# Start and counting stage of a graph network kernel: one load queue, multiplications of zeros ahead of x, bases looked at first, the common path right behind the branch, windows of eleven nodes

## The chip, the core and the metric

The kernel runs on one core of one Trainium2 chip. The metric is the device time of one execution in microseconds (us); of the kernel before, three timed runs and one profiled execution are given. Times inside the execution are counted from the start of the profiled span. PE is the matrix engine (PEld its weight loads), DVE the vector engine, ACT the scalar engine, POOL the GpSimd engine and SP the engine that issues most DMAs.

## What is computed

1250 nodes carry 1024 features; 40000 edges (src, dst, type 0 or 1) are sorted by dst. Two graph networks run one after the other, both in float32. Cut to what matters:

```python
# block 0: norm, relational convolution with two edge types, elu, projection, residual
xn  = ln_w * x * rsqrt(mean(x**2) + 1e-6)
out = xn @ W_root + bias                      # 1024 -> 286
for r in range(2):
    w    = (edge_type == r)
    msg  = (xn[src] @ W_rel[r]) * w
    out += segment_sum(msg, dst) / max(segment_sum(w, dst), 1)
x = layernorm(x + x + elu(out) @ wo)
# block 1: layernorm, 1024 -> 512 -> 256, three rounds of h += f(h + segment_sum(h[src], dst)),
#          256 -> 512 -> 1024, layernorms
```

Both blocks gather over the same edges. The kernel therefore counts the edges once into a dense matrix `adj` (source node by destination node, one plane for each type) and multiplies with it.

## The kernel before

The nodes are cut into T = 10 tiles of P = 125. The first stage does two things side by side on PE:

- **Projection.** For each tile, the eight 128-wide blocks of x are transposed (`turn`, L723), ACT copies them out of PSUM with the weight `lnw` (`weigh`, L438), and `products(u, v)` (L729) multiplies block u with 858 columns of `w_all` in two halves of 429. The weights come in four quarters of two blocks each (`load_w`, semaphores `w_in[0]` to `w_in[3]`).
- **Counting.** The edges are cut into G = 80 rows of 500, each in two half rows of 250. For each row DVE makes one-hots of the sources (`lows`, `oh_low`) and of source block, type and destination (`codes`, `oh_code`, L1126), PE multiplies them (`count`, L715, four matmuls, 240 columns each), and DVE adds the two results to `adj` at the columns of the half row's least destination (L1181 and L1185, loaded into registers by `bases`, L1154). The window behind that base has W = 12 nodes, C = T * W, R * C = 240 columns. Whether every half row fits its window is looked at on the chip (`gaps`, `signs`, L1143 to L1148) and gives `bign`; if one does not, DVE and later PE take another path over `adj_x`, the same matrix in plain float32.

The order of the start is written out by hand. SP issues x of tile 0, `lnw8`, quarter 1 of the weights, dst, src, type, quarters 2 and 3, and x of tile 1; ACT issues quarter 0. POOL makes the iotas `iota_r`, `iota_i`, `iota_c` and then zeroes parts of `adj`; DVE makes `ident`, `iota_l` and its own parts of `adj`, then works on the edges as they land: least dst of each half row (L1087), `e_low` (L1092), `e_code` (L1097), greatest dst (L1099). PE transposes tile 0 and runs `products(0..7, 0)`; ahead of `products(6, 0)` it transposes `e_low`, and ahead of `products(7, 0)` x of tile 1, `e_code` (L708) and the bounds (L780). DVE then copies `edge`, `mini`, `ends` (L1104 to L1107), makes the one-hots of rows 0 and 1, looks at the windows (L1143 to L1149), loads `bign` (L1334) and branches (L1335): the body of `If(big > 0)` stands first in the program and the usual path behind `Else`. What follows both, up to the loop over chunks, stands behind the two.

In the loop over pairs of tiles (`tile_of_1` on PE and on DVE, `Fori(0, T // 2 - 1)`, four passes) each tile has nine count rows. PE's order is row u, products u, for u from 0 to 7; behind row 4 it transposes the next x and has row 5 at once. DVE does rows in order and ahead of its u = 3 the two `y_lo` instructions of the tile before (`low_part`, L1164, L1165). PE waits for one-hots (`onehots`), DVE for counts (`counts_mm`); both are two rows apart through two buffers. When DVE is done it sets `adj_done` (L1225), SP then issues `cb_b`, and the aggregation begins (L864 and L866, single pass float32r).

Of the kernel before, what the change touches and what calls it, by code (L numbers as in the profile page):

```python
# [25 lines left out]
P = 125  # L26
# [9 lines left out]
J = 4  # L36
# [5 lines left out]
W = 12  # L42
# [14 lines left out]
def graph_kernel(nc, x, src, dst, typ, ln_w, w_rel, w_root, conv_b, wo, g_in, b_in, w1, b1, w2, b2,  # L57
                 wa, ba, wb, bb, ng, nb, wd1, bd1, wd2, bd2, g_out, b_out, out):
    with ExitStack() as ctx:
# [113 lines left out]
        def spread(a):  # L173
# [11 lines left out]
        lnw_ps, lnw_set, lows_ready, far_copied, ends_set, far_ready = (  # L185
            sem("lnw_ps"), sem("lnw_set"), sem("lows_ready"), sem("far_copied"), sem("ends_set"), sem("far_ready"))
# [73 lines left out]
        def _(sp):  # L260
# [3 lines left out]

            load_x(0, 0)
            sp.dma_start(lnw8[:], ln_w.rearrange("(k p) -> k p", p=128)).then_inc(lnw_in, 16)
# [87 lines left out]
        def _(pool):  # L354
# [347 lines left out]
        def _(pe):  # L702
# [54 lines left out]

            pe.wait_ge(small_set, 4)
# [4 lines left out]
            turn(1, 0)  # L763
            for u in range(KD):
# [290 lines left out]
        def _(dve):  # L1055
# [4 lines left out]
            dve.memset(zero[:], 0.0).then_inc(small_set, 1)  # L1060
            dve.memset(mini[:], 0)
            dve.memset(edge[:], 0.0)
            dve.memset(farC[:], 0.0).then_inc(prep, 1)
            dve.wait_ge(iotas, 2)
            dve.tensor_scalar(ident[:], iota_r[:], iota_i[:, 0:1], None, ALU.is_equal).then_inc(small_set, 1)
            dve.tensor_copy(iota_l[:], iota_r[0:P].rearrange("p (n o) -> p n o", o=1).broadcast_to([P, LOW, JH]))
            dve.wait_ge(small_set, 4)
            for b in range(5):
# [18 lines left out]
            dve.tensor_reduce(bounds[:, 0:H], halves(dst_i), AX.X, ALU.min)  # L1087
            dve.wait_ge(src_in, 16)
# [402 lines left out]
```

## Time and profile before

| | us |
|---|---|
| three timed runs, median (lowest to highest) | 604.26 (603.21 to 604.66) |
| profiled execution, device time | 605.02 |
| its span | 603.2 |
| PE busy in the span | 574.2 |
| DVE busy | 393.1 |
| ACT busy | 213.8 |
| POOL busy | 103.0 |

The profiled execution is 0.76 us above the median of the runs; 1.8 us of it lie outside the span. Busy times are modelled for PE, since matmuls are pipelined: the time from one start to the next is the better measure of what one costs. In the slices of the profile each of the 40 digits stands for 15.1 us.

### The profile page before, as it was taken

The page shows a single profiled execution, that of the slowest core. Times are in us where ns is not written, and L with a number is a line of the kernel's source. Part 1 is how long each engine was busy: PE and PEld are TensorE (multiplying, and loading weights), DVE is VectorE, ACT ScalarE, POOL GpSimd, SP SyncE. Part 2 cuts the span into 40 slices and gives each one's busy share as a digit, 9 for nine tenths or more (in the row PEclk, how much of TensorE's full clock was granted, in tenths as well). Part 3 has the DMA queues.
Part 4 walks back from the last instruction along what each step waited for, and adds up shares of the span by engine and source line. Part 5 has one row for each costly group of instructions (what it writes and reads, how often), then busy time and mean ns, then how long its engine had stood idle before and what let it go on. Part 6 is the DMA issues. An engine that isn't in the chain of part 4 may idle for free.

```text
span 603.2 us, 8370 instructions
## 1 busy us (share of the span) xinstructions
PE 574.2 (95%) x2575; PEld 395.9 (66%) x2575; DVE 393.1 (65%) x998; ACT 213.8 (35%) x456; POOL 103.0 (17%) x98
## 2 busy tenths in 40 slices
PE   4969999999999999999999999999999999999992
PEld 2535555555558686766788888886877867455540
DVE  7569999999985788888733202015848848655454
ACT  6612233222312446465322222002223224175555
POOL 9300000000000000003054333400211230041230
PEclk9979999999999999999999999999999999999997
DMA  9401111001103121114720000320010100021223
GB/s 259 134 11 35 34 34 35 13 21 34 34 1 89 35 69 35 61 43 118 213 93 0 1 0 0 115 105 1 1 36 0 35 0 2 1 68 34 70 68 102
DMA packets 20848, 30.73 MB, mean 51 GB/s; under 512 B 5393, under 2 KB 15107, under 8 KB 20816
## 3 DMA queue, kind: packets, MB, share of 16 engines
q1 hardware_dynamic: 19846, 29.19, 16.5%
q10 hardware_dynamic: 970, 1.13, 0.7%
q8 instruction: 17, 0.28, 0.2%
q14 instruction: 15, 0.12, 0.1%
HBM read 25.20 MB, written 5.12 MB: 50 GB/s over the span
## 4 chain that ended last, share of the span: by engine, by line
PE 86%; DVE 5%; issue 3%; DMA 2%; DVEq 2%; ACT 1%; POOL 0%; ACTq 0%
PE banks L729 16%; PE banks L918 12%; PE banks L1004 11%; PE banks L835 11%; PE banks L805 5%; PE banks L715 5%; PE banks L940 4%; PE banks L930 4%; PE banks L864 4%; PE banks L866 4%; PE banks L845 3%; PE banks L994 3%; PE banks L809 2%; DVEq L1154 1%; PE banks L820 1%
## 5 line engine op out<-in xcount | busy, mean ns | idle before, releaser
L729 PE MATMUL banks<-w_all,xnT 128*125 128x429 f32 x320 | 131.9, 537 | 2.0 <-DMA w_all<-in_L_gnn_W_rel 2.0
L729 PEld LDWEIGHTS banks<-w_all,xnT 128*125 128x125 f32 x320 | 55.7, 193 | 34.5 <-issue 31.4
L835 PE MATMUL banks<-hT,w_s 128*128 128x250 f32 x320 | 68.7, 375 | 0.4 <-DVE hT L1309 0.3
L835 PEld LDWEIGHTS banks<-hT,w_s 128*128 128x128 f32 x320 | 60.3, 189 | 9.1 <-issue 2.2
L715 PEld LDWEIGHTS banks<-oh_code,oh_low 125*128 125x128 bf16 x320 | 30.7, 98 | 43.9 <-issue 29.1
L715 PE MATMUL banks<-oh_code,oh_low 125*128 125x240 bf16 x320 | 48.3, 273 | 7.8 <-DVE oh_code L1126 7.8
L864 PE MATMUL banks<-y_hi,adj 125*125 125x288 f32 x200 | 55.2, 304 | 0.4 <-DVE small L1225 0.4
L866 PE MATMUL banks<-y_lo,adj 125*125 125x286 f32 x200 | 53.6, 295 | 0.0
L1126 DVE TENSOR_TENSOR oh_code<-iota_c,edge 125x960 bf16<-125x960 f16 x82 | 53.3, 650 | 0.0
L375 POOL TENSOR_SCALAR xh<-x_first,small 125x1024 f32<-125x1024 f32 x6 | 7.4, 1236 | 261.1 <-DVE adj L1253 261.0
L1309 DVE TENSOR_SCALAR hT<-banks,g_c,b_c 128x125 f32<-128x125 f32 x60 | 19.4, 399 | 45.6 <-PE banks L820 45.2
L918 PE MATMUL banks<-adj,h_hi 125*128 125x250 f32 (+1 forms) x180 | 48.2, 366 | 0.0
L918 PE MATMUL banks<-adj,h_lo 125*128 125x250 f32 (+1 forms) x180 | 45.6, 353 | 0.0
L1181 DVE TENSOR_TENSOR adj<-adj,banks 125x240 f32 x80 | 32.1, 401 | 18.2 <-PE banks L715 13.0
L1004 PE MATMUL banks<-wd_s,dT 128*125 128x512 f32 x96 | 42.7, 592 | 0.0
L864 PEld LDWEIGHTS banks<-y_hi,adj 125*125 125x125 f32 x200 | 37.1, 186 | 7.2 <-issue 6.1
L438 ACT ACTIVATE xnT<-banks,lnw 128x125 f32<-128x125 f32 x80 | 22.6, 377 | 52.5 <-PE banks L723 52.5
L380 POOL TENSOR_TENSOR h_lo<-h,h_hi 125x256 fp32r<-125x256 f32 x30 | 21.8, 732 | 107.6 <-ACT h_hi L570 107.6
L866 PEld LDWEIGHTS banks<-y_lo,adj 125*125 125x125 f32 x200 | 37.3, 186 | 0.0
L805 PE MATMUL banks<-wo_s,yT 128*125 128x512 f32 x80 | 36.0, 592 | 0.0
L1122 DVE TENSOR_TENSOR oh_low<-iota_l,edge 125x512 bf16<-125x512 f16 x82 | 34.3, 418 | 0.2
L918 PEld LDWEIGHTS banks<-adj,h_hi 125*128 125x128 f32 x180 | 29.8, 189 | 5.5 <-issue 1.4
(187 smaller groups left out, 912.2 us busy)
## 6 DMA issues: line engine op xcount, KB each, us to landing
xt<-in_x SPq DMA_DIRECT2D x15, 448.0 KB
out_x<-ot SPq DMA_DIRECT2D x9, 448.0 KB
w_s<-in_L_gnn_W SPq DMA_DIRECT2D x5, 512.0 KB, 6.1
xn<-in_x SPq DMA_DIRECT2D x5, 448.0 KB
wd_s<-in_L_gnn_Wd SPq DMA_DIRECT2D x1, 2048.0 KB, 12.8
w_all<-in_L_gnn_W_rel SPq DMA_DIRECT2D x6, 286.0 KB, 8.6
wo_s<-in_L_gnn_wo_weight SPq DMA_DIRECT2D x1, 1024.0 KB, 6.6
w_all<-in_L_gnn_W_root SPq DMA_DIRECT2D x3, 286.0 KB, 7.9
```

Source lines behind the costliest of these rows:

```text
L715: ins = pe.matmul(pb[:, b, q * R * C:(q + 1) * R * C], oh_low[:, b, q, :, j], oh_code[:, b, q, :, j], start=(j == 0), stop=(j == JH - 1))
L729: ins = pe.matmul(pb[0:P, 2 + 2 * v + n, 0:FH], xnT[:, u], w_all[:, u, n * FH:(n + 1) * FH], start=(u == 0), stop=(u == KD - 1))
L805: pe.matmul(pb[0:P, 5 + q], yT[:, i], wo_s[:, i, q * 512:(q + 1) * 512], start=(i == 0), stop=False)
L835: ins = pe.matmul(pb[:, 4 + f % 2, 0:2 * P], w1_s[:, k, f * 128:(f + 1) * 128], hT[:, k], start=(k == 0), stop=(k == KD - 1))
L864: pe.matmul(pb[0:P, b + r, 0:F + 2], mine, y_hi[:, s, r * (F + 2):(r + 1) * (F + 2)].bitcast(kind), start=(s == 0), stop=False)
L866: ins = pe.matmul(pb[0:P, b + r, w0:w0 + F], mine, y_lo[:, s, r * F:(r + 1) * F].bitcast(kind), start=False, stop=(s == T - 1))
L918: ins = pe.matmul(pb[:, 3 * f + c, 0:n], part[:, s, f * 128:(f + 1) * 128], adj[:, 0, s, c0:c0 + n], start=(s == 0 and part is h_hi), stop ...
L930: ins = pe.matmul(pb[:, 3 * f + c, 0:n], wa_s[:, k, f * 128:(f + 1) * 128], zT[:, k, c0:c0 + n], start=(k == 0), stop=(k == K2 - 1))
L1004: ins = pe.matmul(pb[0:P, 2 + 2 * u + q], (dT, dT_odd)[c % 2][:, k, u * P:(u + 1) * P], wd2_s[:, k, q * 512:(q + 1) * 512], start=(k == 0) ...
L1122: return dve.tensor_tensor(oh_low[:, b], both(iota_l, LOW), spread_out(edge[:, 0], g, LOW), ALU.is_equal)
L1126: return dve.tensor_tensor(oh_code[:, b], both(iota_c, R * C), spread_out(code, g, R * C), ALU.is_equal)
L1181: dve.tensor_tensor(place, place, window(b, 0), ALU.add).then_inc(first_added, 1)
```

## The change

- **Loads.** SP issues all first loads, in the order `lnw8`, x of tile 0, quarters 0 and 1, dst, src, type, quarters 2 and 3, x of tile 1. ACT issues none of them.
- **Zeros on PE.** DVE sets `oh_code[:, 0]` to zero early; PE multiplies it with itself, 5 matmuls of 440 columns ahead of its first waits and 4 more behind the transposes of tile 0.
- **Start of DVE and POOL.** DVE makes `ident` and `iota_l` ahead of the zeroing of `mini`, `edge` and `farC`; POOL waits for `ident` ahead of `iota_c`; DVE zeroes 7 blocks of plane 1 in place of 5, POOL two fewer.
- **Bases first.** The greatest dst comes right behind the least; PE transposes the bounds ahead of `products(5, 0)` into banks 4 and 5; DVE copies `mini` and `ends` and looks at the windows while it waits for PE's transposes of the edges, not behind the first one-hots.
- **Branch.** `bign[0, 1]` says that all windows fit. `If(fine > 0)` has the usual path as its first body, and what followed both bodies (`into_encoder`) stands in each of them.
- **Window.** W is 11 in place of 12: 220 columns in each count matmul, 880 elements in place of 960 for each partition in `codes`, 220 in place of 240 in each addition to `adj`.

```diff
-W = 12
+W = 11
@@ SP
+            sp.dma_start(lnw8[:], ln_w.rearrange("(k p) -> k p", p=128)).then_inc(lnw_in, 16)
             load_x(0, 0)
-            sp.dma_start(lnw8[:], ln_w.rearrange("(k p) -> k p", p=128)).then_inc(lnw_in, 16)
+            load_w(sp, 0)
             load_w(sp, 1)
@@ POOL
+            pool.wait_ge(small_set, 4)
             pool.iota(iota_c[:], ...)
-            pool.wait_ge(small_set, 3)
-            for r, b in [(1, b) for b in range(5, T)] + [(0, 8), (0, 9)]:
+            for r, b in [(1, b) for b in range(7, T)] + [(0, 8), (0, 9)]:
@@ ACT
-            load_w(act, 0)
@@ PE
+            def warm(n, bank):
+                flat = oh_code[:, 0].rearrange("p q c j -> p (q c j)")
+                for _i in range(n):
+                    pe.matmul(pb[:, bank, 0:2 * R * C], flat[:, 0:128], flat[:, 0:2 * R * C], start=True, stop=True)
+            pe.wait_ge(warm_set, 1)
+            warm(5, 5)
             pe.wait_ge(small_set, 4)
             ...
             turn(0, 0)
             turn(1, 0)
+            warm(4, 5)
             for u in range(KD):
...
+                if u == 5:
+                    pe.wait_ge(bounds_ready, 1)
+                    for i in range(2 * H):
+                        ins = pe.transpose(pb[0:1, 4 + i // H, i % H * G:(i % H + 1) * G], bounds[:, i:i + 1], ident[0:G, 0:G])
+                    ins.then_inc(bounds_ps, 1)
...
-                    turn_edges(1, e_code)
-                    for i in range(2 * H):
-                        ins = pe.transpose(pb[0:1, i // H, (J + i % H) * G:(J + i % H + 1) * G], bounds[:, i:i + 1], ident[0:G, 0:G])
-                    ins.then_inc(edges_ps, 1)
+                    turn_edges(1, e_code).then_inc(edges_ps, 1)
@@ DVE
+            dve.memset(oh_code[:, 0], 0.0).then_inc(warm_set, 1)
+            dve.wait_ge(iotas, 2)
+            dve.tensor_scalar(ident[:], ...).then_inc(small_set, 1)
+            dve.tensor_copy(iota_l[:], ...)
             dve.memset(mini[:], 0)
             dve.memset(edge[:], 0.0)
             dve.memset(farC[:], 0.0).then_inc(prep, 1)
-            for b in range(5):
+            for b in range(7):
...
             dve.tensor_reduce(bounds[:, 0:H], halves(dst_i), AX.X, ALU.min)
+            dve.tensor_reduce(bounds[:, H:2 * H], halves(dst_i), AX.X, ALU.max).then_inc(bounds_ready, 1)
...
             dve.reciprocal(small1[:, 4:5], small1[:, 2:3]).then_inc(xn_rstd, 1)
+            dve.wait_ge(bounds_ps, 1)
+            (copies of mini and ends, then gaps, signs)
+            dve.tensor_scalar(bign[0:1, 1:2], signs[0:1, 0:1], 0.0, None, ALU.is_ge)
+            dve.tensor_scalar(bign[0:1, 0:1], signs[0:1, 0:1], 0.0, None, ALU.is_lt).then_inc(big_ready, 1)
             dve.wait_ge(edges_ps, 1)
             (copies of edge; the one-hots of rows 0 and 1; the look at the windows is gone from behind them)
...
-            with dve.If(big > 0):
-                dve.memset(adj_x[:], 0.0).then_inc(wide_set, 1)
-                ...
-            with dve.Else():
-                counted(adj)
-                after_counts()
-                aggregated(adj)
-            (the common lines up to adj_full)
+            fine = dve.value_load(bign[0:1, 1:2], min_val=0, max_val=1)
+            with dve.If(fine > 0):
+                counted(adj)
+                after_counts()
+                aggregated(adj)
+                into_encoder()
+            with dve.Else():
+                dve.memset(adj_x[:], 0.0).then_inc(wide_set, 1)
+                ...
+                into_encoder()
```

## Rows read from the trace of the kernel before

**Rows 1.** The page: the final chain by engine, and the costliest group of additions (count, busy, mean ns)

```profile
PE 86%; DVE 5%; issue 3%; DMA 2%; DVEq 2%; ACT 1%; POOL 0%; ACTq 0%
...
L1181 DVE TENSOR_TENSOR adj<-adj,banks 125x240 f32 x80 | 32.1, 401 | 18.2 <-PE banks L715 13.0
```

**Rows 2.** Chain of waits, 0 to 46 us: start, length, what (DVEq: its sequencer)

```profile
2.19 7.70 DMA w_all<-in_L_gnn_W_rel
...
10.03 10.93 PE banks L729 x24
20.96 0.40 PE banks L708 x4
...
23.67 0.29 PE banks L780 x4
...
23.98 0.89 DVE edge L1104 x2
...
25.53 0.42 DVE oh_low L1122
...
27.42 0.23 DVE gaps L1143
...
29.18 0.03 issue
...
30.26 2.84 issue
...
34.22 0.10 DVE adj L1181
...
35.89 0.98 PE banks L715 x4
...
43.36 0.43 PE banks L715 x4
```

**Rows 3.** Timeline of PEld, 13 to 14 us: start, length, instruction, idle before it

```profile
13.02 0.33 PEld L729 LDWEIGHTS banks<-w_all,xnT 128*125 128x125 f32 x1 [0.38 <-issue]
13.74 0.33 PEld L729 LDWEIGHTS banks<-w_all,xnT 128*125 128x125 f32 x1 [0.38 <-issue]
```

**Rows 4.** Stretches: length; busy PE, PEld, DVE, ACT, POOL; granted clock, DMA share, GB/s

```profile
15.00:16.00 1.00, 1.00 (x4) 0.56 (x3) 0.99 (x2) 1.00 (x2) 1.00 (x2) 1.00 1.09 367
...
35.00:41.00 6.00, 5.11 (x13) 2.75 (x14) 5.15 (x13) 0.00 (x0) 0.00 (x0) 0.50 0.00 0
42.00:46.00 4.00, 4.00 (x24) 2.67 (x23) 3.22 (x10) 1.13 (x4) 0.00 (x0) 1.00 0.03 6
```

**Rows 5.** DMA, 8.84 to 8.90 us (issue; us to landing) and 31.0 to 31.5 us (queue; packets)

```profile
w_all<-in_L_gnn_W_rel SPq DMA_DIRECT2D x1, 286.0 KB, 10.4
...
q14 instruction: 1, 0.01, 6.2%
```

**Rows 6.** Timeline of 0 to 24 us, POOL and DVE

```profile
1.13 3.05 POOL L359 IOTA iota_c<- 125x480 f16 x1
...
2.40 1.85 DVE L1065 TENSOR_SCALAR ident<-iota_r,iota_i 128x128 f32<-128x128 f32 x1
...
12.09 0.67 DVE L1087 TENSOR_REDUCE bounds<-dst_i 80x2 f32<-80x500 int32 x1 [2.34 <-DMA dst_i<-in_dst]
...
17.65 0.14 DVE L1101 RECIPROCAL small<-small 125x1 f32<-125x1 f32 x1
```

**Rows 7.** Timeline around and inside the loop, and a DVE row at 323.93 us

```profile
29.32 1.61 PE L729 MATMUL banks<-w_all,xnT 128*125 128x429 f32 x4
...
39.34 0.66 DVE L1165 SCALAR_TENSOR_TENSOR y_lo<-banks,small,y_hi 125x429 f32 x1
...
109.31 0.65 DVE L1126 TENSOR_TENSOR oh_code<-iota_c,edge 125x960 bf16<-125x960 f16 x1
...
110.02 0.60 PE L715 MATMUL banks<-oh_code,oh_low 125*128 125x240 bf16 x4 [0.24 <-DVE oh_code L1126]
...
323.93 1.35 DVE L1309 TENSOR_SCALAR hT<-banks,g_c,b_c 128x125 f32<-128x125 f32 x4 [14.25 <-PE banks L820]
```

More of the change, by code:

```diff
@@ L1060, in _ @@
             dve.memset(zero[:], 0.0).then_inc(small_set, 1)
+            dve.memset(oh_code[:, 0], 0.0).then_inc(warm_set, 1)
+            dve.wait_ge(iotas, 2)
+            dve.tensor_scalar(ident[:], iota_r[:], iota_i[:, 0:1], None, ALU.is_equal).then_inc(small_set, 1)
+            dve.tensor_copy(iota_l[:], iota_r[0:P].rearrange("p (n o) -> p n o", o=1).broadcast_to([P, LOW, JH]))
             dve.memset(mini[:], 0)
@@ L1096, in _ @@
                 part = slice(q * JH * P, (q + 1) * JH * P)
-                dve.scalar_tensor_tensor(e_code[:, part], dst_i[:, part], bounds[:, q:q + 1], e_mark[:, part],
-                                         ALU.subtract, ALU.add)
-            dve.tensor_reduce(bounds[:, H:2 * H], halves(dst_i), AX.X, ALU.max).then_inc(edges_ready, 1)
+                ins = dve.scalar_tensor_tensor(e_code[:, part], dst_i[:, part], bounds[:, q:q + 1], e_mark[:, part],
+                                               ALU.subtract, ALU.add)
@@ L1100, in _ @@
+            ins.then_inc(edges_ready, 1)
             dve.wait_ge(xn_sd, 1)
             dve.reciprocal(small1[:, 4:5], small1[:, 2:3]).then_inc(xn_rstd, 1)
-            dve.wait_ge(edges_ps, 1)
-            for f in range(2):
-                dve.tensor_copy(edge[:, f, 0:G], pb[0:P, f, 0:J * G].rearrange("p (j g) -> p g j", j=J))
-            dve.tensor_copy(mini[:].rearrange("o (g q) -> o q g", q=H)[:, :, 0:G],
-                            pb[0:1, 0, J * G:(J + H) * G].rearrange("o (q g) -> o q g", q=H))
@@ L1107, in _ @@
-            dve.tensor_copy(ends[:].rearrange("o f (g q) -> o f q g", q=H),
-                            pb[0:1, 0:2, J * G:(J + H) * G].rearrange("o f (q g) -> o f q g", q=H)).then_inc(codes_ready, 1)
+            dve.wait_ge(bounds_ps, 1)
+            dve.tensor_copy(mini[:].rearrange("o (g q) -> o q g", q=H)[:, :, 0:G],
+                            pb[0:1, 4, 0:H * G].rearrange("o (q g) -> o q g", q=H))
+            step(dve.tensor_copy(ends[:].rearrange("o f (g q) -> o f q g", q=H),
+                                 pb[0:1, 4:6, 0:H * G].rearrange("o f (q g) -> o f q g", q=H)))
@@ new lines, in _, with sift @@
+            crowds = [0]
+            def sift(ins):
+                ins.then_inc(crowd, 1)
+                crowds[0] += 1
+                dve.wait_ge(crowd, crowds[0])
+            NG = G * H
+            NS = NG - SPAN
+            dve.memset(gaps[0:1, NG - 1:NG], 0.0)
+            dve.tensor_tensor(gaps[0:1, 0:NG - 1], ends[0:1, 0, 1:NG], ends[0:1, 0, 0:NG - 1], ALU.subtract)
+            dve.scalar_tensor_tensor(gaps[0:1, NG:NG + NS], ends[0:1, 0, SPAN:NG], -float(W), ends[0:1, 0, 0:NS], ALU.add, ALU.subtract)
@@ new lines, in _ @@
+            sift(dve.scalar_tensor_tensor(gaps[0:1, NG + NS:2 * NG + NS], ends[0:1, 0], float(W - 1), ends[0:1, 1], ALU.add, ALU.subtract))
+            dve.tensor_reduce(signs[0:1, 1:2], gaps[0:1, NG + NS:2 * NG + NS], AX.X, ALU.min)
+            sift(dve.tensor_reduce(signs[0:1, 0:1], gaps[0:1, 0:2 * NG + NS], AX.X, ALU.min))
+            dve.tensor_scalar(bign[0:1, 1:2], signs[0:1, 0:1], 0.0, None, ALU.is_ge)
+            dve.tensor_scalar(bign[0:1, 0:1], signs[0:1, 0:1], 0.0, None, ALU.is_lt).then_inc(big_ready, 1)
@@ L1109, in _ @@
+            dve.wait_ge(edges_ps, 1)
+            dve.tensor_copy(edge[:, 0, 0:G], pb[0:P, 0, 0:J * G].rearrange("p (j g) -> p g j", j=J))
+            dve.tensor_copy(edge[:, 1, 0:G], pb[0:P, 1, 0:J * G].rearrange("p (j g) -> p g j", j=J)).then_inc(codes_ready, 1)
             dve.wait_ge(codes_ready, 1)
```

55 lines of the change are left out of this document (19 added, 36 removed).

## Prediction

> **What bounds the kernel now.** I read the page's chain first: PE holds 86% of it [rows 1], so only time in which PE waits, runs at its low clock level or does needless columns can be won, and whatever is won early moves everything behind it. Then the chain of waits over the first 46 us [rows 2], to see where PE is not the one that works. Three places stand out. First, PE's first product starts at 10.03, when quarter 0 of the weights has landed (2.19 + 7.70 = 9.89). Second, from 23.98, when DVE begins to copy the turned edges, the chain is DVE's up to 35.89, when PE gets the one-hots of count row 2. The largest piece in it, 2.84 us from 30.26, is no instruction at all. PE has nothing left from about 30.9 on (the last products of row 1 start at 29.32 and take 1.61 [rows 7]). Third, the clock: two loads of weights in the first products are 0.72 apart [rows 3], yet 24 records took 10.93 in all, which is 0.46 each, so the clock rose on the way; the clock column shows no half level there, the spacing does. Behind the idle 5 us it shows 0.50 (1.2 GHz) over the whole of 35 to 41 us, and 1.00 (2.4 GHz) from 42 on [rows 4]. Inside the loop PE is the bound but for one place a tile: row 5 comes right behind row 4, and PE gets it at 110.02, as DVE's codes end (109.31 + 0.65 = 109.96) [rows 7].
>
> **Loads and zeros.** In one queue quarter 0 no longer shares the DMA engines with quarter 1. The engines carry 367 GB/s while SP alone feeds them [rows 4], so one queue is enough to fill them. Quarter 0 is 858 KB and x is 500 KB; at that rate they take 3.8 us, so with the start at about 2.2 and one to two us of completion quarter 0 lands between 7 and 9, not at 9.89. But the bytes of all loads together are unchanged, and the last piece of quarter 3 landed at 8.85 + 10.4 = 19.25 (it is the issue of that window) [rows 5], against the 20.96 at which PE is ready for block 6 [rows 2]. So of this part at most 20.96 - 19.25 = 1.7 us can reach the end: what is late next is quarter 3. The first x is issued behind `lnw8` and nothing from ACT runs beside it, for which I add 0.3: block 6 at 19.6, a gain of 1.4 (bounds: -0.3, if PE starts no earlier, to 2.0). The nine multiplications of zeros cost at most 9 x 440 columns at 1.2 GHz = 3.3 us of PE, five while it would wait for x, four while ACT copies xnT and quarter 0 is under way; if that cover failed (quarter 0 in ahead of the last of them) they would cost PE up to 1.5 us, which the slack before quarter 3 takes up. What they win in clock is hidden by the same wait: I book nothing for it.
>
> **DVE's and POOL's start.** `ident` took 1.85 us and ended at 4.25, as POOL's `iota_c` did (1.13 + 3.05 = 4.18) [rows 6]: it was held, not working. Now POOL waits for it, so `ident` is early; but the 3.05 of `iota_c` then run beside `iota_l` and the zeroing, and such a hold (up to 1.6, what `ident` took over 0.25 or so) may only move there. The zeroing grows by two blocks, which I put at 1 us each from the element count; DVE has 2.34 of idle ahead of L1087 [rows 6]. So dst is met 0 to 1.5 late. The Trainium skill (GPSIMD Engine Reference, the table of section 1) says that POOL shares its SBUF interfaces with DVE, in conflict with DVE's two-port modes or two SBUF inputs; the trace agrees with the 1.85 of `ident`, and by the rule the upper end, 1.5 late, is the one to expect. From there to `e_code` and the reciprocal it takes 17.79 - 12.09 = 5.7, so up to 19.3, and the look at the bases (below, 2.4) ends by 21.7; its cover is PE, which hands over the edges at 22.3. No cost, with 0.6 us to spare.
>
> **Bases first.** From block 6 to the hand-over PE took 23.98 - 20.96 = 3.02; the four transposes of the bounds (0.29) [rows 2] go to block 5, ahead of quarter 3's landing, so 2.73 stay: DVE starts copying at 19.6 + 2.73 = 22.35, not 23.98. A gain of 1.65. Off DVE's path there go the copies of `mini` and `ends` (24.87 to 25.53: 0.66) and the look (27.42 to 29.18: 1.76).
>
> **The branch.** From 30.26 DVE does nothing for 2.84 us, behind L1335 and ahead of the loop, and in that time the queue of instruction reads moves one packet [rows 2, 5]: it jumps over the body of `If` and the code there has to be read. With the usual path first nothing is jumped over. I take 0.0 for it (bounds 0.0 and 2.84). The Trainium skill has the rule (Runtime: NRT & Kernel Launch, Instruction fetch mechanics: reading ahead is sequential, and a taken branch out of the window waits for a DMA), and the trace agrees with its 2.84. The jump is not gone: it stands behind `into_encoder` now, over the other body. There DVE waits 14.25 us for PE [rows 7], which hides it; without that cover it would cost its 2.84.
>
> **Eleven nodes.** A count of 240 columns takes 0.43 for four matmuls [rows 2]; 20 columns less at 2.4 GHz are 0.008 each, 0.033 a row (bounds 0, if the loads of weights set the spacing, and 0.036, a twelfth). A twelfth of `codes` (0.65) [rows 7] would be 0.054 and of an addition (0.401) [rows 1] 0.033; both have a fixed part, so I take 0.04 and 0.02: a DVE row gets 0.08 shorter (0 to 0.12).
>
> **Sum to row 5 of tile 1.** DVE from first copy to first addition: 34.22 - 23.98 = 10.24, less 0.66, 1.76, 2.84 and 0.08 for two shorter codes = 4.9. So the first addition comes at 27.25, not 34.22. Row 2's codes end 1.6 later (35.84 - 34.22, less 0.08, rounded): PE gets row 2 at 28.85, not 35.89. PE itself needs until some 28.6 for rows 0 and 1 with their products (what ended at 30.93, earlier by 1.65 and by the copies of 0.66): it stands still for 0.2 or 0.3 us, not 5, and the 6 us at half clock [rows 4] go as well. From there DVE sets the pace: three rows of 1.5 and the two `y_lo` instructions (0.66 and about 0.2) give row 5 at 28.85 + 4.5 + 0.85 = 34.2. Before it was 43.36 [rows 2]. **9.2 us.**
>
> **Sum from there.** In each of seven more tiles three count rows and two DVE rows lie between PE's count 2 and count 5, where DVE is the slower: 2 x 0.08 = 0.16 there, and 7 x 0.033 = 0.23 on the other rows: 0.39 x 7 = 2.7. The last 12 rows give 0.4. **3.1 us** (bounds 1.2, if only DVE gets shorter, and 4). Behind the loop nothing changes but positions in the program.
>
> 12.3 us in all. The profiled execution of 605.02 becomes 592.7; it lies 0.76 above the median, so the median of 604.26 becomes **592.0**.
>
> **Rivals.**
> A, the forecast: 592.0, by itself 589.5 to 594.3 (loads -1.4 or +0.4, window 1.2 or 4). Chance 0.72.
> B, the wait at the branch stays (the loop's head has to be read in any case). PE then stands 3.1 us: +2.8, and if the clock falls behind that, as it did behind 5 us, half of the 6 us again: 594.8 to 597.6. For it: the 2.84 is only known next to a taken branch. Against: the next instruction is the next in sequence. 0.12.
> C, a back edge of DVE's loop has to read code. Before there was no such wait in the loop. The body moves inside the program, and where it crosses one block of code more than is kept, each of three back edges costs 2.84, less its lead over PE of half a row or so, 0.8: +6, 598. 0.06.
> D, loads: the single queue brings quarter 3 or x of tile 1 later, or DVE is held beyond its spare 0.6: each us is one us, 593 to 596. 0.07.
> E, slower: windows of eleven are too few. A single half row of 250 edges that reaches over 12 nodes decides it: `fine` is 0, everything takes the `adj_x` path. That is 20 blocks of zeros more (some 20 us) and 400 aggregation matmuls in plain float32: a float32 matmul of 429 columns is two records of 0.36 (half of 0.72 [rows 3]), so one of 288 is 0.48, against 288 columns at 2.4 GHz, 0.12, in one pass: +144. About 750 us. Against: 32 edges a node make 250 edges span eight nodes, and over the reference's dst the largest distance inside a half row is 9, where 10 are allowed. 0.01. The remaining 0.02 is for gains lost in ways I don't see, to within 0.3% of before.
>
> **How the numbers follow.** The range of 589.3 to 597.6 takes in A, B and D, over 8 in 10. A measurement of this kernel tells 0.3% (1.8 us) from no change. All cases but E and the remainder are faster: 0.96; same 0.02; slower 0.02, which gives E a little for mishaps like it.
>
> **What would show it.** In the profile after: quarter 0's landing and the first product (8 to 9 us), and PE waiting for quarter 3 close to 19.5; `edge` copied at 22.3, the look at the bases ahead of it; no gap of 2.84 before the first addition to `adj`, at 27.2; row 2's count at 28.9 with a clock of 1.00 throughout; a tile of the loop 0.4 shorter than before; no idle PE where DVE jumps behind `into_encoder`. The forecast is wrong if DVE meets dst after 14, if instruction reads appear in the loop, or if a half clock shows between 28 and 35 us.

## The result: 593.0 us, forecast 592.0

The changed kernel took 593.0 us (592.87 to 594.06, four runs), the kernel before beside it 604.04: a ratio of 0.982, interval 0.9807 to 0.9832. The profiled execution was the longest of the four, 594.06 with a span of 592.0; the span before was 603.2, so the traces have 11.2 us to share out.

The page after, its final chain, the queues of instruction reads and two of the groups that the window of eleven nodes touches (the additions to `adj` answer to [rows 1]):

```profile
q14 instruction: 15, 0.12, 0.1%
...
PE 86%; DVE 4%; DMA 2%; issue 2%; DVEq 2%; SPq 1%; ACT 1%; POOL 0%
...
L715 PE MATMUL banks<-oh_code,oh_low 125*128 125x220 bf16 x320 | 44.7, 260 | 2.8 <-DVE oh_code L1159 2.8
...
L1196 DVE TENSOR_TENSOR adj<-adj,banks 125x220 f32 x80 | 30.6, 383 | 15.1 <-PE banks L715 14.1
```

The timeline of PE up to the copies of the edges, which answers to the first part of [rows 2] (start, length, instructions, idle time before them):

```profile
2.11 2.02 PE L762 MATMUL banks<-oh_code 125*128 125x440 bf16 x5 [2.11 <-DVE oh_code L1072]
...
7.19 1.63 PE L762 MATMUL banks<-oh_code 125*128 125x440 bf16 x4
8.84 3.12 PE L729 MATMUL banks<-w_all,xnT 128*125 128x429 f32 x8
12.17 3.15 PE L729 MATMUL banks<-w_all,xnT 128*125 128x429 f32 x8 [0.21 <-DMA w_all<-in_L_gnn_W_rel]
16.43 1.68 PE L729 MATMUL banks<-w_all,xnT 128*125 128x429 f32 x4 [1.11 <-DMA w_all<-in_L_gnn_W_rel]
...
19.87 0.66 PE L708 MATMUL banks<-ident,e_low 80*125 80x80 f32 x4
```

Behind the zeros eight matmuls of the products take 3.12 us, 0.39 each and not the 0.72 of [rows 3], so they run at 2.4 GHz from the first on; but PE then stands twice, because it now meets the quarters of the weights as they land. The next answer is the chain of waits from the copies of the edges on, which answers to the second part of [rows 2]:

```profile
22.88 0.49 DVE edge L1140
23.37 0.41 DVE edge L1141
23.80 0.04 DVE oh_low L1155
...
23.90 0.55 DVEq L1367
24.45 0.32 DVE oh_code L1159
...
24.81 0.57 PE banks L715 x4
```

There is no pause of 2.84 us any more, and L1367, the load of the branch's flag into a register, is done by DVE's sequencer at 24.45, while the one-hots still run. The clock over the stretch that stood at 0.50 before [rows 4] (length; busy time of PE, PEld, DVE, ACT, POOL; granted clock, DMA share, GB/s):

```profile
28.00:34.00 6.00, 5.78 (x30) 3.36 (x29) 5.64 (x15) 1.47 (x5) 0.00 (x0) 1.00 0.13 42
```

**Where the 11.2 us come from.** Two instructions cut the span into three parts: the start of DVE's fifth addition (DVE adds twice for each row; the first of the two is counted, so this is that of row 4. PE begins row 5 of tile 1 behind it, 0.05 us in the changed kernel and 0.20 in the kernel before) and that of the eightieth, in the last row. Up to the fifth it is 43.16 before and 33.79 after: 9.37 gained. From the fifth to the eightieth 138.76 and 137.07: 1.69 gained. From the eightieth to the end of the span 421.28 and 421.14: 0.14. The forecast had 9.2, 3.1 and 0. This is one trace of each kernel: in a second one of the changed kernel the span is 591.2 and the fifth addition starts at 32.75, so the gain up to it is 10.4 there and 12.0 in all.

### The profile page after: what moved, and what is told of

Same layout as the page of the kernel before. It is cut to its first block, busy times and chain, and to the rows that moved or that the text cites. A ratio compares the mean times of both kernels' runs of the same rounds, so it can differ in the third digit from the quotient of the medians.

```text
span 592.0 us, 8385 instructions
## 1 busy us (share of the span) xinstructions
PE 571.5 (97%) x2584; PEld 394.8 (67%) x2584; DVE 391.1 (66%) x1002; ACT 213.9 (36%) x456; POOL 100.8 (17%) x90
## 4 chain that ended last, share of the span: by engine, by line
PE 86%; DVE 4%; DMA 2%; issue 2%; DVEq 2%; SPq 1%; ACT 1%; POOL 0%
PE banks L729 14%; PE banks L929 12%; PE banks L1015 12%; PE banks L846 12%; PE banks L816 5%; PE banks L715 5%; PE banks L951 4%; PE banks L941 4%; PE banks L875 4%; PE banks L877 4%; PE banks L856 3%; PE banks L1005 3%; PE banks L820 2%; DVEq L1169 1%; DMA w_all<-in_L_gnn_W_rel 1%
## 5 line engine op out<-in xcount | busy, mean ns | idle before, releaser
L729 PE MATMUL banks<-w_all,xnT 128*125 128x429 f32 x320 | 129.1, 526 | 1.3 <-DMA w_all<-in_L_gnn_W_rel 1.3
L729 PEld LDWEIGHTS banks<-w_all,xnT 128*125 128x125 f32 x320 | 53.8, 188 | 31.8 <-issue 30.8
L1159 DVE TENSOR_TENSOR oh_code<-iota_c,edge 125x880 bf16<-125x880 f16 x82 | 50.0, 610 | 0.0
L715 PE MATMUL banks<-oh_code,oh_low 125*128 125x220 bf16 x320 | 44.7, 260 | 2.8 <-DVE oh_code L1159 2.8
L1196 DVE TENSOR_TENSOR adj<-adj,banks 125x220 f32 x80 | 30.6, 383 | 15.1 <-PE banks L715 14.1
L438 ACT ACTIVATE xnT<-banks,lnw 128x125 f32<-128x125 f32 x80 | 22.6, 378 | 43.7 <-PE banks L723 43.7
```

The source lines that it names most:

```text
L715: ins = pe.matmul(pb[:, b, q * R * C:(q + 1) * R * C], oh_low[:, b, q, :, j], oh_code[:, b, q, :, j], start=(j == 0), stop=(j == JH - 1))
L729: ins = pe.matmul(pb[0:P, 2 + 2 * v + n, 0:FH], xnT[:, u], w_all[:, u, n * FH:(n + 1) * FH], start=(u == 0), stop=(u == KD - 1))
L1159: return dve.tensor_tensor(oh_code[:, b], both(iota_c, R * C), spread_out(code, g, R * C), ALU.is_equal)
L1196: dve.tensor_tensor(place, place, window(b, 0), ALU.add).then_inc(first_added, 1)
```

## The experiments

All are edits to the changed kernel, but for one to the kernel before; "neither" and the last row undo or change two things at once, the others one. The table gives the timed median, the ratio to the kernel before on the same chip with its interval, and from each trace the start of the edges' first copy, of the fifth addition, and the time from the fifth to the eightieth.

| kernel | us (lowest to highest) | ratio | copy | fifth | to 80th |
|---|---|---|---|---|---|
| before | 604.04 | 1 | 23.98 | 43.16 | 138.76 |
| changed | 593.0 (592.87-594.06) | 0.982 [0.9807, 0.9832] | 22.88 | 33.79 | 137.07 |
| changed, again | 594.08 (593.2-595.01) | 0.9841 [0.9822, 0.9859] | 21.83 | 32.75 | 137.04 |
| old branch order | 594.56 (594.15-595.45) | 0.9843 [0.9824, 0.9862] | 21.37 | 34.48 | 136.31 |
| bases looked at late | 597.3 (596.52-597.96) | 0.9879 [0.9861, 0.9897] | 22.30 | 37.66 | 137.05 |
| window of twelve | 595.74 (595.3-596.07) | 0.9856 [0.9839, 0.9874] | 21.50 | 32.61 | 139.63 |
| before + branch order | 600.98 (600.69-601.82) | 0.9947 [0.9928, 0.9966] | 24.37 | 39.28 | 138.97 |
| no zeros | 593.34 (592.86-593.99) | 0.9826 [0.9812, 0.9839] | 23.06 | 33.97 | 137.02 |
| two queues | 593.01 (592.66-593.06) | 0.982 [0.9806, 0.9833] | 22.35 | 33.26 | 137.05 |
| neither | 594.25 (593.71-595.53) | 0.9845 [0.9825, 0.9865] | 23.51 | 34.43 | 137.04 |
| shifted loop | 593.02 (591.42-596.06) | 0.9825 [0.9798, 0.9853] | 22.53 | 33.44 | 136.36 |
| shifted loop, again | 592.24 (591.6-593.08) | 0.9805 [0.9787, 0.9823] | 21.75 | 32.66 | 136.33 |
| subtraction at row 6 | 590.6 (590.19-593.33) | 0.9781 [0.9766, 0.9795] | 24.67 | 35.22 | 134.62 |
| the same, twelve | 593.16 (592.52-594.68) | 0.9825 [0.9805, 0.9844] | 21.27 | 32.00 | 137.26 |

How to read it: the last column repeats to 0.05 us (six traces of the loop as it is in the changed kernel gave 137.02 to 137.07), so it settles tenths. The column of the copies does not: with the start of the program unaltered it lies between 21.27 and 24.67, since the first loads land when they will (`dst` is met at 11.97 to 14.05). What an edit does between copy and fifth addition is therefore read as their difference, 10.91 in the changed kernel (33.79 - 22.88), 10.92 in its repeat (which was expected at 592.7 to 593.3 us and took 594.08). The ratios are coarser: the changed kernel itself gave 0.982 on one chip and 0.9841 on another, 1.3 us apart, so a difference of two ratios from different chips that is smaller than this says little by itself.

**The branch's order undone.**

```diff
-            fine = dve.value_load(bign[0:1, 1:2], min_val=0, max_val=1)
-            with dve.If(fine > 0):
-                counted(adj)
+            big = dve.value_load(bign[0:1, 0:1], min_val=0, max_val=1)
+            with dve.If(big > 0):
+                dve.memset(adj_x[:], 0.0).then_inc(wide_set, 1)
...
+            with dve.Else():
+                counted(adj)
```

> The changed kernel with the order of the branch put back (wide body first, usual path behind Else, common lines behind both); all else as changed. Theory 1 (the 2.84 us is the read of code behind a taken branch, and DVE sets the pace from its first addition to row 5): the gap of 2.8 us is back ahead of the first addition (26.4 becomes 29.2 us), PE waits some 2 us for row 2 at full clock, row 5 comes 2.6 us later than 33.84; 593.0 becomes 595.6. Theory 2 (the gap of before only existed because the sequencer had waited for the windows to be looked at; now it runs ahead and the read of code hides behind the one-hots): 593.0 to 594.0. Theory 3 (the wait is long enough for the clock to fall): 598 or more.

The chain of waits of this kernel, from the jump (L1350) to the first addition:

```profile
23.30 0.07 DVEq L1350
23.37 0.13 issue
23.50 0.61 DVE oh_code L1159
24.11 2.07 issue
26.18 0.05 DVEq L1207
...
27.30 0.10 DVE adj L1196
```

The gap is back at the same place with everything else in the new form, 2.07 us here. But it is only the part that nothing covers: DVE's sequencer jumps ahead of the second codes, is done with that at 23.37, and its next step is at 26.18, 2.81 us later; 0.74 of it lie beside the one-hots. In the kernel before it was 2.84 (30.26 to 33.10) and all of it bare, since the flag came last. So the jump has the same price in both, and what is seen of it depends on what DVE still has queued. From the copy to the fifth addition it is 13.11 instead of 10.91: 2.2 us. But the loop is 0.76 shorter than the changed kernel's, 136.31 against 137.07; 2.2 - 0.76 = 1.4, and the two ratios differ by 0.0023, 1.4 us (by 0.0002 with the repeat's ratio). The mechanism is the first theory's, the clock did not fall, and its 595.6 us was too high: part of the jump is covered, which the second theory had for the whole of it, and the loop is shorter. The jump's cost is shown in the trace; that the new order also costs something in the loop was not in either theory, and led to the shifted loop below.

**The branch's order alone, in the kernel before** (the same edit the other way round, with `bign`'s second flag).

> The kernel before with the order of the branch alone changed. Theory 1 (2.84 us of reading code go; PE's idle stretch of 5 us shrinks to 2.1 and the clock stays at 1.00, so DVE and no longer PE's half clock sets row 5): row 5 at 38.5 in place of 43.36, 604.0 becomes 599.2. Theory 2 (the clock falls all the same): 2.84 only, 601.2. Theory 3 (the read of code is only moved): 604.0.

From copy to fifth addition 14.91, where the kernel before has 19.18: 4.27 gained in the trace, against 3.2 us in the time (604.77 x (1 - 0.9947)), of an interval of 2.1 to 4.4. Of the 4.27, 2.78 are at the first addition (31.83 - 24.37 = 7.46 behind the copy instead of 10.24) and 1.49 between it and the fifth, since PE stands still for so much less that its clock stays up. That is the first theory; its row 5 at 38.5 came at 39.39, and the time, 600.98, is nearer to the second theory's 601.2, whose fallen clock the trace does not have. Below are PE's row 2 and the window around it, in this kernel:

```profile
33.75 0.60 PE L715 MATMUL banks<-oh_code,oh_low 125*128 125x240 bf16 x4 [2.44 <-DVE oh_code L1126]
```

```profile
30.00:35.00 5.00, 2.56 (x11) 1.25 (x10) 3.02 (x8) 1.23 (x3) 0.00 (x0) 1.00 0.17 64
35.00:40.00 5.00, 4.14 (x24) 2.60 (x23) 4.93 (x14) 1.13 (x4) 0.00 (x0) 1.00 0.02 5
```

**The look at the bases put back behind the one-hots.** The bounds' transposes stand behind the codes' again, and copies, `gaps` and `signs` where they stood:

```diff
-                if u == 5:
-                    pe.wait_ge(bounds_ready, 1)
...
-                    turn_edges(1, e_code).then_inc(edges_ps, 1)
+                    turn_edges(1, e_code)
+                    for i in range(2 * H):
+                        ins = pe.transpose(pb[0:1, 4 + i // H, i % H * G:(i % H + 1) * G], bounds[:, i:i + 1], ident[0:G, 0:G])
+                    ins.then_inc(edges_ps, 1)
```

> The changed kernel with the bounds transposed behind the edges again, mini and ends copied behind edge, and the look at the windows behind the one-hots of rows 0 and 1. Theory 1 (each piece lies on DVE's path to the first addition, and the sequencer can no longer load bign ahead): 0.3 for PE's transposes, 0.66 for the copies, 1.8 for the look, 1.1 for the load of bign behind it = 3.8 us later at the first addition, of which 1 us was spare on PE's side at row 2 but none at row 5: 596.5 to 596.8. Theory 2 (the sequencer's part overlaps in either order): 2.7 us, 595.7.

PE's row 2 in this kernel, and then the window around it:

```profile
31.69 0.91 PE L715 MATMUL banks<-oh_code,oh_low 125*128 125x220 bf16 x4 [2.56 <-DVE oh_code L1137]
32.41 2.78 PE L729 MATMUL banks<-w_all,xnT 128*125 128x429 f32 x4
```

```profile
30.00:35.00 5.00, 3.31 (x8) 1.78 (x9) 4.75 (x13) 0.00 (x0) 0.00 (x0) 0.66 0.02 5
```

It took 597.3 us, where the theories had 596.5 to 596.8 and 595.7. The timed difference to the changed kernel is 0.0059, 3.6 us; in the traces the way from copy to fifth addition is 15.36 instead of 10.91, 4.45 longer, and the loop is the same. The first addition comes 7.80 behind the copy (30.10 - 22.30) instead of 3.53: 4.27 of the 4.45 are there already, near the 3.8 of the first theory. The copies of `mini` and `ends` and the look are 0.6 and 1.8 of them; the other 1.9 are the load of the flag, the branch and the load of the bases, which ran beside the one-hots in the changed kernel and now stand behind the look. PE is idle for 2.56 us ahead of row 2, and here the clock does fall: the count takes 0.91 instead of 0.56 and the four matmuls behind it 2.78 instead of 1.61. That is 1.5 us of PE, but little of it is new: from the first to the fifth addition it takes 7.56 us, and 7.18 in the kernel with the old branch order, where the clock stays up and DVE sets the pace. So the fallen clock cost some 0.4. The look is worth more than its own length (2.4 with the copies) above all because the sequencer's work behind it gets covered too.

**The window of twelve nodes** in the changed kernel (`W = 12`).

> The changed kernel with windows of twelve nodes. Theory 1 (0.027 a row on PE, and next to nothing on the stretch where DVE sets the pace, since its sequencer does): 1.6 us in the loop and 0.1 or 0.2 ahead of it, 594.7 to 594.8. Theory 2 (the prediction's term of 3.1 us was right and something else took 1.5 us of it back): 596.1.

The loop takes 139.63 instead of 137.07, 2.56 us. The ratios differ by 0.0036, 2.2 us, and the time, 595.74, lies between the two theories. The 2.56 is less than the 3.1 of the forecast, and it is 0.87 more than the 138.76 of the kernel before, which has the same window. So two things had happened to that term at once: it was set 0.5 too high, and something in the loop took 0.87 back.

**The loop shifted by sixteen instructions.** They do nothing and stand where DVE waits for PE in any case:

```diff
+            for k in range(16):
+                dve.memset(gaps[0:1, 2 * NG + NS + k:2 * NG + NS + k + 1], 0.0)
             dve.wait_ge(edges_ps, 1)
```

> The changed kernel with sixteen one-element zeroings on VectorE ahead of its wait for the codes' transposes, where it idles 1.64 us: they do nothing but move everything behind them, the counting loop too, by sixteen instructions in VectorE's program. In the changed kernel every second tile takes 16.54 us instead of 16.40, and VectorE's sequencer pauses 0.12 us more between two rows of it, at row 3; with the branch's old order the same loop takes 16.40 us for all tiles. First theory (the pause is the crossing from one fetched block of instructions to the next, and lies at the one row where VectorE has no slack): shifted by sixteen instructions it falls more than a row earlier, where VectorE waits for TensorE anyway, all pitches become 16.40, row 5 of tile 1 to the end of the counting shortens from 138.6 to about 137.9 us, and the time is 592.1 to 592.5. Second theory (the odd and even tiles differ for another reason, as the buffers that they use): pitches and time stay, 592.7 to 593.3 us. Third: the shift brings the crossing to a worse place, 593.5 or more, which would speak for the first theory's mechanism too.

> The changed kernel with the sixteen one-element zeroings ahead of the counting loop, a second time, because its first timing was scattered (591.4 to 596.1 us) while its trace had all pitches at 16.40 us and 0.72 us less from row 5 of tile 1 to the last addition. First theory (the trace is right and the 0.72 us reaches the end): 592.0 to 592.5 us, ratio to the kernel before 0.001 below the unaltered changed kernel's. Second (what is gained in the loop is waited for again behind it): the same as the unaltered one within 0.2 us.

The chain of waits in the fourth tile, first of the changed kernel, then of the shifted one, from PE's row to the sequencer's last step ahead of DVE's addition (L1194 and L1196 there are L1196 and L1198 here):

```profile
78.70 0.41 PE banks L715 x4
...
79.14 0.04 DVEq L1194
79.18 0.17 issue
79.35 0.05 DVEq L1196
```

```profile
78.00 0.41 PE banks L715 x4
...
78.43 0.04 DVEq L1196
78.47 0.05 issue
78.52 0.05 DVEq L1198
```

The pause of 0.17 between these two steps of the sequencer is 0.05 in the shifted kernel. At row 5 PE's idle time shows what becomes of it, in the same order of kernels:

```profile
83.56 0.56 PE L715 MATMUL banks<-oh_code,oh_low 125*128 125x220 bf16 x4 [0.33 <-DVE oh_code L1159]
```

```profile
82.72 0.57 PE L715 MATMUL banks<-oh_code,oh_low 125*128 125x220 bf16 x4 [0.20 <-DVE oh_code L1161]
```

The tiles of the loop now take 16.39 to 16.42 us, where every second took 16.51 to 16.54 and the second tile 16.76. In that one the pause at the same step is longer:

```profile
46.00 0.41 issue
```

This is 0.36 more than 0.05, and with 0.12 in each of the three passes behind it makes 0.72. The way to the eightieth addition is 136.36 and 136.33: 0.72 us less, in both traces, for sixteen instructions that compute nothing. The loop's position in the program is what matters; the rival about buffers falls, as the buffers were left as they were. The pause itself is not gone in the shifted kernel: it stands at another step now, nearly two rows earlier (L1202 to L1161, 0.21 us instead of 0.07 ahead of 75.19, and so in each later pass; 0.46 in the first, ahead of 42.63), where it costs nothing. In the times the two measurements, 0.9825 and 0.9805, stand against 0.982 and 0.9841 of the unaltered kernel: in the mean 0.0016 or 0.9 us lower, but the intervals overlap, so the times alone would not have shown it (593.02 misses the 592.1 to 592.5 of the first theory, 592.24 meets its 592.0 to 592.5). That the pause is the step from one block of fetched code to the next, the first theory, fits with its moving by a fixed number of instructions, and with its being longer in the first pass, in which reads of 8 KB each move (q14: 0.12 MB in 15; packets at 42.5 and 47.1). But none moves in the fourth tile, so the cause was not shown, only the dependence on position.

**The subtraction ahead of row 6.**

```diff
-                    if u == 3:
+                    if u == 6:
                         low_part(t - 1, 1 - v)
```

> The changed kernel with one edit inside the counting loop: VectorE subtracts the high parts of tile t (low_part) ahead of row 6 of the next tile instead of ahead of row 3. In the changed kernel TensorE idles 0.20 us (odd tiles) to 0.56 and 0.33 us (even tiles) ahead of row 5, because VectorE is behind by then. First theory (the two subtractions of 0.4 and 0.6 us meet VectorE with the least slack at row 3, and later in the tile they would be hidden): the stall ahead of row 5 goes, row pitch stays 1.85 us, 0.2 to 0.33 us for each of 8 tiles, 2.0 to 2.3 us in all, 590.7 to 591.0 us. Second theory (VectorE's work of a tile is what sets the pace, wherever it stands): the stall moves to row 8 of the tile or to row 0 of the next, and the time stays at 592.7 to 593.3. Third (the products of the next tile wait for y_lo, so that a late subtraction makes TensorE wait): slower, 594 or more.

This is the fastest kernel: 590.6 us, although its profiled execution met the latest loads of all. The loop takes 134.62 instead of 137.07, 2.45 us less, and from the copy to the fifth addition it is 10.55 instead of 10.91. This is the first theory, with its time (590.7 to 591.0). The stretch from 40 to 160 us of the changed kernel, and the same of this one:

```profile
40.00:160.00 120.00, 117.88 (x554) 70.32 (x553) 106.33 (x282) 35.69 (x105) 0.00 (x0) 1.00 0.10 30
```

```profile
40.00:160.00 120.00, 120.00 (x566) 71.45 (x565) 110.17 (x292) 35.70 (x105) 0.00 (x0) 1.00 0.10 30
```

PE has no idle time left there, so the wait did not move to another row: two subtractions of 0.4 and 0.7 us stood at the one place where DVE had no slack.

**The same with a window of twelve.**

> The changed kernel with the subtraction ahead of row 6 (as in the variant that took 590.6 us and left TensorE no idle time in the counting) and, besides, the window of twelve nodes again. In the unaltered changed kernel the window of twelve cost 2.6 us from row 5 of tile 1 on. First theory (the window's worth is TensorE's: a count of 0.43 instead of 0.40 us per row, 75 rows left, and nothing of VectorE's since it has slack here): 75 x 0.027 = 2.0 us more than the variant with eleven, 592.5 to 592.9 us. Second (VectorE's longer additions and one-hots, 0.1 us a row, run into the bound again with twelve): 593.1 us or more, with idle time of TensorE back in the rows ahead of row 5 or 8.

137.26 against 134.62: 2.64 us, 0.0044 or 2.7 us in the ratios. PE is never idle in either, so all of it is PE's, and my number for the first theory was too low: I had taken 0.027 us per row from two rounded pitches, while 2.64 over 75 rows is 0.035. That is four matmuls of 20 columns at 2.4 GHz, 0.033, as the forecast had it. The longer instructions of DVE cost nothing of their own; the second theory falls, with its time met.

**The start: no zeros, two queues, neither.** The first leaves L762 and its zeroed operand out. The second puts the loads back:

```diff
-            sp.dma_start(lnw8[:], ln_w.rearrange("(k p) -> k p", p=128)).then_inc(lnw_in, 16)
             load_x(0, 0)
-            load_w(sp, 0)
+            sp.dma_start(lnw8[:], ln_w.rearrange("(k p) -> k p", p=128)).then_inc(lnw_in, 16)
             load_w(sp, 1)
...
+            load_w(act, 0)
```

> The changed kernel without TensorE's multiplications of zeros ahead of and behind the transposes of x (TensorE idles instead). First theory (TensorE waits for the DMA of each quarter of the weights in any case, and the third quarter's landing sets when the edges' transposes run): the first products run at the half clock, 0.72 us each instead of 0.36, for some us, but TensorE has 1.1 us of idle time ahead of quarter 2 and 0.7 ahead of quarter 3, which takes most of it up: 592.8 to 593.3 us. Second theory (half-clock products delay the look at the bases, or TensorE comes late to quarter 3): edge copies 1 to 2 us later and the same in the time, 594 to 595 us.

> The changed kernel with the first quarter of the weights fetched by ScalarE's queue again, the rest by SyncE's, as before the change. First theory (one queue lets the quarters land in the order in which they are wanted, and the third one earlier; the prediction put this at 1.4 us at block 6 of the first tile): edge copies 1 to 1.4 us later, 594.0 to 594.4 us. Second theory (the DMA engines share the same bytes either way, and what the first kernel lost was the order of x and the edge arrays, not the second queue): within 0.3 us of the changed kernel, 592.7 to 593.3.

> The changed kernel with both edits at its start undone: the first quarter of the weights on ScalarE's queue again, and no multiplications of zeros. Undone one at a time they cost nothing that could be measured (593.3 and 593.0 us). First theory (each makes up for the other's lack: with two queues the quarters land early but x is late and its products start at the half clock; with one queue TensorE waits for quarters in any case): without both, the first products start near 10.0 us at the half clock, the low codes' transposes run 1 to 1.4 us later than with both, and the time is 593.7 to 594.4 us. Second theory (neither has an effect on the start): within 0.3 us of the unaltered one.

Taken out alone, neither costs anything that can be measured (0.9826 and 0.982 against 0.982). For the zeros this is the first theory; for the queues it is the second theory's number, but what makes up for the second queue is the zeros. With two queues PE is handed x later, at 6.02 us instead of 5.47, but then runs from 9.24 to its sixth block without a wait for a quarter. Without zeros and with one queue its first products are slow, and what is lost was waiting time ahead of the quarters that follow. What caps the start with either edit is the last quarter: it is in at 19.83 (changed), 19.92 (no zeros) and 19.30 (two queues), and the low codes' transposes run 0.04, 0.04 and 0.10 behind it. With neither edit it is in at 18.31 and PE is not there before 20.60, since its products start late and slow: the first theory's mechanism. PE and PEld of the kernel with neither:

```profile
9.56 9.45 PE L730 MATMUL banks<-w_all,xnT 128*125 128x429 f32 x20 [1.57 <-DMA w_all<-in_L_gnn_W_rel]
...
20.60 0.56 PE L709 MATMUL banks<-ident,e_low 80*125 80x80 f32 x4
```

```profile
11.12 0.34 PEld L730 LDWEIGHTS banks<-w_all,xnT 128*125 128x125 f32 x1 [0.38 <-issue]
11.83 0.33 PEld L730 LDWEIGHTS banks<-w_all,xnT 128*125 128x125 f32 x1 [0.38 <-issue]
```

and the same transposes in the repeat of the changed kernel:

```profile
18.92 0.56 PE L708 MATMUL banks<-ident,e_low 80*125 80x80 f32 x4
```

The loads of weights are 0.71 us apart, 0.72 in [rows 3], so PE is at the half clock, and the low codes' transposes run at 20.60 instead of 18.92, 1.7 us later, and 1.68 later is the fifth addition. (Against the first trace of the changed kernel, 19.87, it is only 0.7.) Measured from where DVE meets `dst`, so that the loads' own shift falls out, the copy of the edges comes 11.87 us behind it in this kernel, 11.89 and 12.53 in the two with the old start, and 9.03 to 10.62 in all eleven others. But the times, 594.25 against 594.08 of the unaltered kernel beside it, do not show the 1.7 us. In the profiled executions 0.9 of it is left (spans of 592.0 and 591.2). Part is given back at the end, and by an edit: below is the issue of the last store from ACT, in the changed kernel and in the one with neither.

```profile
588.19 1.30 ACTq L699 DMA_DIRECT2D out_x<-ot  x2
```

```profile
588.78 1.12 ACTq L700 DMA_DIRECT2D out_x<-ot  x2
```

In the ten traces in which ACT issues none of the first loads, the span ends 3.84 to 3.87 us behind the last work of ACT and DVE, and an instruction read moves 2.2 us behind that work; in the four in which it issues quarter 0 (before, its branch order, two queues, neither) it ends 3.28 to 3.40 behind it, and no read moves there. So the one queue costs some 0.5 us at the end, which the start gained by it has to pay for; that it is ACT's program standing elsewhere fits, and was not tested. Whether the start is worth over a microsecond in the time stays open; that the two edits stand in for each other up to the copy of the edges is shown in the traces.

## Why the prediction was right, step by step

**Loads.** Right, in the term that was booked. Block 6 was put at 19.6 and is at 19.87 in the one trace, 18.92 in the other; quarter 0 was put between 7 and 9 and the first product runs at 8.84 and 8.50; the copies were put at 22.35 and are at 22.88 and 21.83. The reason given, one queue, is only half of it: the same is had with two queues and zeros. "I book nothing for it", the sentence on the zeros, holds with one queue and would not hold with two. "What is late next is quarter 3" is right: it is in at 19.83 and 18.67 against the 19.25 of the forecast.

**DVE's and POOL's start.** The hold was expected to move to the zeroing, up to 1.5 us. The timelines of DVE and POOL, which answer to [rows 6]:

```profile
1.97 0.16 DVE L1074 TENSOR_SCALAR ident<-iota_r,iota_i 128x128 f32<-128x128 f32 x1
...
2.21 2.83 POOL L362 IOTA iota_c<- 125x440 f16 x1 [1.04 <-DVE ident L1074]
...
3.15 8.47 DVE L1081 CAST adj<-zero 125x1274 fp32r<-125x1274 f32 x7
...
12.85 0.67 DVE L1099 TENSOR_REDUCE bounds<-dst_i 80x2 f32<-80x500 int32 x1 [0.80 <-DMA dst_i<-in_dst]
...
18.55 0.15 DVE L1114 RECIPROCAL small<-small 125x1 f32<-125x1 f32 x1
```

`ident` takes 0.16 instead of 1.85, with POOL quiet. The seven blocks took 8.47, 1.2 each where I had 1.0, and DVE was through at 12.05, so it came 0 late: it waited 0.80 for `dst` itself. The reciprocal is at 18.55 (bound 19.3), and the look ends at 21.24 (bound 21.7), 1.64 ahead of the edges. No cost, as forecast, though the loads landed later here; no run undoes this edit alone, so its own share is not known. The upper end of 1.5, which the sentence on the Trainium skill (GPSIMD Engine Reference, the table of section 1) pointed to, did not come.

**The branch.** The gap went to 0.0, the value taken; undone, it costs 2.2 us up to the fifth addition, and 2.07 of its 2.81 are bare. What I had missed is a second gain: the register load of the flag (0.55), and what the sequencer does around it (29.18 to 30.26 in the kernel before), now run beside the one-hots, so the first addition comes at 26.41, 3.53 behind the copy, and not 4.9 behind it (27.25 - 22.35). The rule of the Trainium skill (Runtime: NRT & Kernel Launch, Instruction fetch mechanics), that a taken branch out of what has been read ahead waits for a fetch, agrees with both kernels that jump, at 2.84 and 2.81. The jump behind `into_encoder` is hidden, as forecast; the row that answers to the last of [rows 7]:

```profile
312.17 1.04 DVE L1324 TENSOR_SCALAR hT<-banks,g_c,b_c 128x125 f32<-128x125 f32 x3 [14.25 <-PE banks L831]
```

**Row 2 and row 5.** Row 2 was put at 28.85 and is at 28.94, though DVE had its codes at 27.95: PE itself, with what it has to do for rows 0 and 1, is not there before. Row 5 was put at 34.2 and is at 33.84:

```profile
28.94 0.56 PE L715 MATMUL banks<-oh_code,oh_low 125*128 125x220 bf16 x4
...
33.84 0.57 PE L715 MATMUL banks<-oh_code,oh_low 125*128 125x220 bf16 x4 [0.22 <-DVE oh_code L1159]
```

The clock stayed at 1.00, and rival B is out. That the two numbers meet is partly luck. From the copy of the edges to row 5 the forecast has 34.2 - 22.35 = 11.85 and the traces have 10.96: 0.9 too long, half of it ahead of row 2 (the flag) and half behind it, where "From there DVE sets the pace" fails at first, as DVE is a microsecond ahead of PE at row 2. In the first trace the loads came 0.5 late and hid most of this; in the repeat row 5 is at 32.79, 1.4 before the forecast.

**From row 5 on.** This is the term that was wrong: 3.1 us forecast, 1.69 found. Of the missing 1.4, 0.5 is the sentence "2 x 0.08 = 0.16 there, and 7 x 0.033 = 0.23 on the other rows". Tiles shrink by nine times 0.033, 0.30 each (16.71 to 16.41 between the kernels of twelve and eleven nodes), and not by 0.39: where DVE is behind, PE's idle time went from 0.24 to only 0.19 to 0.22 (but for the pause), so DVE's shorter instructions bought next to nothing. The larger part, 0.87, is the last sentence of that paragraph, "Behind the loop nothing changes but positions in the program": in the loop the position changed too, and that costs 0.72 of it (shown by the shift, and by the old branch order with 0.76). Of the remaining 0.15, 0.1 is that the kernel before took 16.61 for its second tile and 16.7 for the others. Rival C, code that has to be read at a back edge, did not come: instruction reads do move in the first pass of the loop, which the forecast named as a sign of being wrong, but they do so in the kernel before too (43.7 and 50.8 there, 42.5 and 47.1 here), and what they may cost is the 0.41 of the second tile, not 2.84 for each back edge. The bounds of the term, 1.2 to 4, held it. Behind the loop positions count too: the end costs 0.5 more with one queue, and 0.7 was gained ahead of that, which was not traced; the 0.14 left is near the 0 of the forecast by their cancelling.

**The total.** 9.4 and 1.7 instead of 9.2 and 3.1, so the traces give 11.2 where 12.3 was forecast (12.0 with the repeat). The medians give 604.04 - 593.0 = 11.0, and the changed kernel's lies 1.0 above the forecast.

## What to carry to other kernels

Ask of every edit on the way to a loop what stands behind it: the look at the bases was 2.4 us long with its copies, and taking it off the path was worth 4.45 in the traces and 3.6 in the time, since the load of the flag and the sequencer's work behind it then ran beside the one-hots. Ask the same of a jump: 2.81 us of it cost 2.07 where DVE had a codes instruction queued. Where an engine is the bound but for one row in nine, look for the small instructions that stand in that row: moving two of them by three rows gave 2.4 us, nearly as much as all of the narrower window. And a program's layout is a parameter, of the loop as of the end; when a tile's time alternates between two values, shift the loop by a few idle instructions before looking for a deeper cause.

## What the hardware showed that I had not expected

- A sequencer's pause of 0.12 us (0.17 instead of 0.05) at a fixed place of DVE's program, in every second tile, that moves to another step when the loop is shifted by sixteen instructions; it becomes 0.13 of idle PE (0.33 against 0.20) only because it falls into the one row without slack.
- PE's clock fell after pauses of 1.10 and then 2.56 us in one kernel and held after 1.15 and then 2.44 in another, at the same point of the program. Idle length alone does not tell; what decides was not settled here.
- The first loads land up to 2.1 us apart in executions of programs with the same start (`dst` met at 11.97 and at 14.05), and 0.9 us apart in two of the same program (12.85 and 11.98), while the 75 rows of the loop repeat to 0.05 us. It is why the parts of the start, at 1 to 2 us, had to be read in the traces.
- The span ends 3.84 to 3.87 us behind the last work of ACT and DVE in the ten traces of kernels whose first loads all come from one queue, and 3.28 to 3.40 behind it in the four where ACT issues some of them.
- A taken branch of DVE over an `If` body took its sequencer 2.84 and 2.81 us in two kernels, of which instructions queued ahead of it cover what they can: none and 0.74.
